# GpSimd multiplies four of the twelve FFN weight units by their signs

## The reference

```python
x = x + 0.5 * ffn(layernorm(x), w_gate_up, w_proj)
x = x + attn(layernorm(x), Wq, Wk, Wv, Wo)      # 32 heads, sliding window of 128
x = x + 0.5 * ffn(layernorm(x), w_gate_up, w_proj)

def ffn(x, w_gate_up, w_proj):                  # 4096 x 512 and 512 x 2048
    gate, up = split(x @ ternary(w_gate_up).T)
    return rms_norm(silu(gate) * up) @ ternary(w_proj).T

def ternary(w):                                 # groups of 64 along a row, in bf16
    scale = clip(mean(abs(w)), 1e-8)            # of each group
    return clip(round(w / scale), -1, 1) * scale
```

## Time and profile before

| | us |
|---|---|
| median of 3 runs | 2083.98 (2083.1 to 2087.64) |
| the profiled execution | 2085.55 |
| its span, first to last instruction | 2083.7 |
| TensorE busy | 1959.7 (94%) |
| VectorE busy | 1637.6 (79%) |
| ScalarE busy | 1471.2 (71%) |
| GpSimd busy | 803.3 (39%) |

### The profile page before, as it was taken

One profiled execution on the slowest core, in us unless ns is written; L12 is line 12 of the kernel. 1 busy time (PEld: TensorE's weight loads), 2 busy tenths in 40 slices (PEclk: granted clock), 3 DMA queues, 4 the chain that ended last, 5 costly groups with the idle time before them and its releaser, 6 DMA issues. The chain is left out here.

```text
span 2083.7 us, 61746 instructions
## 1 busy us (share of the span) xinstructions
PE 1959.7 (94%) x24766; PEld 1429.4 (69%) x25022; DVE 1637.6 (79%) x4144; ACT 1471.2 (71%) x2617; POOL 803.3 (39%) x688
## 2 busy tenths in 40 slices
PE   6578799999999999999999999999999999999778
PEld 4355577777777777777777777777777777777466
DVE  7956788778877888778887888878887888878774
ACT  7746777677776777767776777767776777777672
POOL 1124334443444344444443444444434443433321
PEclk9789899999999999999999999999999999999889
DMA  6324766566665566656774567557664566646650
GB/s 208 132 41 74 122 104 115 93 108 113 121 120 85 102 111 113 113 90 121 118 119 82 97 113 128 107 89 121 120 104 87 103 124 111 115 85 113 117 108 21
DMA packets 760878, 222.23 MB, mean 107 GB/s; under 512 B 745744, under 2 KB 745744, under 8 KB 760080
## 3 DMA queue, kind: packets, MB, share of 16 engines
q1 hardware_dynamic: 760592, 218.26, 58.4%
HBM read 25.17 MB, written 8.39 MB: 16 GB/s over the span
## 5 line engine op out<-in xcount | busy, mean ns | idle before, releaser
L677 ACT ACTIVATE masked<-masked,exp_bias,exp_scale 128x256 f32<-128x256 f32 (+1 forms) x1024 | 503.8, 562 | 8.6
L988 PEld LDWEIGHTS ps_gu<-xt_A,wgu_t 128*128 128x128 bf16 x8192 | 472.0, 99 | 34.8 <-DVE wgu_t L727 7.6
L988 PE MATMUL ps_gu<-xt_A,wgu_t 128*128 128x128 f16 x8192 | 485.2, 220 | 9.7 <-DVE hid L809 5.1
L988 PE MATMUL ps_gu<-xt_C,wgu_t 128*128 128x128 f16 x8192 | 482.1, 220 | 2.1 <-DMA xt_C<-xh 2.1
L988 PEld LDWEIGHTS ps_gu<-xt_C,wgu_t 128*128 128x128 bf16 x8192 | 467.2, 99 | 11.3 <-DMA xt_C<-xh 2.3
L800 DVE TENSOR_TENSOR prob<-masked,prob 128x1024 f16<-128x1024 f32 (+1 forms) x256 | 355.1, 1387 | 9.1 <-ACT prob L700 9.1
L826 DVE CUSTOM_DVE_ANT_0 masked<-ps_s,mask 128x256 f32<-128x256 f32 (+1 forms) x1024 | 336.9, 384 | 1.0 <-PE ps_s L1035 0.9
L800 DVE TENSOR_TENSOR h_lo<-hid,h_hi 128x512 f16<-128x512 f32 x256 | 198.8, 776 | 129.2 <-ACT h_hi L565 128.4
L565 ACT ACTIVATE h_hi<-hid 128x512 f16<-128x512 f32 x256 | 160.4, 627 | 166.0 <-DVE hid L815 155.8
L534 POOL TENSOR_TENSOR acc_C<-acc_C,sq 128x512 f32<-128x512 f32 x95 | 121.2, 1276 | 396.5 <-ACT sq L694 396.5
L1046 PE MATMUL ps_yy<-wp_t,h_lo 128*128 128x512 bf16 x1024 | 263.7, 380 | 0.0
(11 more groups left out here) (163 smaller groups left out, 2269.9 us busy)
## 6 DMA issues: line engine op xcount, KB each, us to landing
stream<-in_L_attn_x_dram SPq DMA_DIRECT2D x32, 256.0 KB, 3.3
pt<-prob SPq DMA_TRANSPOSE x512, 3.2
out_dram<-stream SPq DMA_DIRECT2D x32, 256.0 KB, 2.7
stream<-in_L_ffn_w_gate_up_dram SPq DMA_DIRECT2D x4, 1024.0 KB, 5.6
prob<-in_L_ffn_w_gate_up_dram SPq DMA_DIRECT2D x4, 1024.0 KB, 6.0
stream<-in_L_ffn_w_proj_dram SPq DMA_DIRECT2D x2, 1024.0 KB, 5.1
prob<-in_L_ffn_w_proj_dram SPq DMA_DIRECT2D x2, 1024.0 KB, 5.0
wv<-in_L_attn_Wo_dram SPq DMA_DIRECT2D x1, 1024.0 KB, 7.9
```

The source lines that it names most:

```text
L677: t = act.activation(p, p, ACT.Exp, bias=exp_bias[:, 4 * g + h:4 * g + h + 1], scale=exp_scale[:, 0:1])
L988: t = pe.matmul(bank[:, j * P:(j + 1) * P], wgu_t[:, k, at:at + P], xt[s][:, part, k, :], start=(k == 0 and part == 0), stop=(k == KD - 1 ...
```

## The change

The product with the signs moves into a function `signed(eng, n)` that either engine can issue. GpSimd does it for units 1, 3, 5 and 7, VectorE for the other eight. GpSimd's four stand in its program between the normalising of block 0 (L498) and the maximum of the scales (L504), and count on a semaphore of their own, `w_qp`. All waits on `w_q` go through `units_done(eng, n)`, which waits for both counts. VectorE gets one wait more, ahead of L714 of units 3, 5, 7 and 9: `w_diff` has two buffers, and GpSimd must have read the one that is written over.

```diff
+        POOL_UNITS = (1, 3, 5, 7)
+
+        def units_done(eng, n):
+            pool_has = sum(u <= n for u in POOL_UNITS)
+            need(eng, w_q, n + 1 - pool_has)
+            need(eng, w_qp, pool_has)
+
+        def signed(eng, n):
+            u = UNITS[n]
+            dst = (wgu_t[:, :, u * 512:(u + 1) * 512] if u < NGU else
+                   wp_t[:, :, (u - NGU) * P:(u - NGU + 1) * P])
+            k = dst.shape[1]
+            eng.wait_ge(w_mk, n + 1)
+            eng.wait_ge(w_sgn, 2 * n + 2)
+            return eng.tensor_tensor(out=dst, in0=w_diff[n % 2].rearrange("p (k c) -> p k c", k=k),
+                                     in1=w_sign[n % 3].rearrange("p (k c) -> p k c", k=k), op=ALU.mult)
 ...
             low(xh[:, 1, :], xhat[:, :], xh[:, 0, :], a_xh["A"], 1, g_xl["A"])
+            for n in POOL_UNITS:
+                signed(pool, n).then_inc(w_qp, 1)
             pool.wait_ge(w_gmax, NGU + 1)
 ...
                 if step == 0:
-                    pool.wait_ge(w_q, NTU)
+                    units_done(pool, NTU - 1)
 ...
                 act.wait_ge(w_tr, i + 1)
-                need(act, w_q, i // 2 - 2)
+                units_done(act, i // 2 - 3)
 ...
                 dve.wait_ge(w_grp, n + 1)
+                if n - 2 in POOL_UNITS:
+                    units_done(dve, n - 2)
                 dve.tensor_tensor(out=diff, in0=wide, in1=w, op=ALU.subtract).then_inc(w_dif, 1)
 ...
-                dve.wait_ge(w_mk, n + 1)
-                dve.wait_ge(w_sgn, 2 * n + 2)
-                (the same product as in signed) .then_inc(w_q, 1)
+                if n not in POOL_UNITS:
+                    signed(dve, n).then_inc(w_q, 1)
 ...
-                        pe.wait_ge(w_q, 2 * c + 2)
+                        units_done(pe, 2 * c + 1)
 ...
-            pe.wait_ge(w_q, NTU)
+            units_done(pe, NTU - 1)
```

More of the change, by code:

```diff
@@ L199, in macaron @@
         w_q = sem("w_q")
+        w_qp = sem("w_qp")
         fs_step = sem("fs_step")
```

## The result

The changed kernel takes 2093.79 us (median, 2093.12 to 2095.25), the kernel before 2083.89 (2081.85 to 2087.64): ratio 1.0043, 95% interval 1.0032 to 1.0054. Slower, as forecast; 2091.3 was predicted, between 2085.8 and 2095.5. The profiled executions differ by less than the medians: spans of 2083.7 and 2091.3 us, +7.6, where +7.3 was predicted.

A forecast was written before the change was run, and what follows sets the result against it. VectorE was taken to bound the weight-unit stage, nearly level with the TensorE, ScalarE, GpSimd loop, and TensorE the steady stage. TensorE's 7.3 us later release, added whole to the 2083.98 us median, gave 2091.3 us, range 2085.8 to 2095.5.

The forecast's parts named there:

- Duration of the product: Each GpSimd sign product of 128x2048 bf16 takes 4.05 us, kept between 3.2 and 4.5.
- Exclusion: In the weight units, GpSimd's products hold VectorE out, making its chain 2.46 + 1.45 + 1.45 + 1.24 = 6.6 us later.
- TensorE: L988's gate products wait for GpSimd's products; the last starts at about 81.86 us instead of 74.57, +7.3 us.
- From there to the end: TensorE's +7.3 us passes through ScalarE to GpSimd's last maximum L511 and VectorE's L761, and the steady stage takes it over whole.
- The rival without exclusion: In the weight units VectorE stays free and only the loop through late TensorE costs: +3.2 us, 2087.2; chance 0.07.
- for whole instructions: VectorE and GpSimd shut each other out on SBUF, each let in only when the other's instruction is over.
- The clock: TensorE's clock may slow unit 7's gate product by 1.1 us or shift start-up stretches; upward 0.10, two stretches less 0.07.
- a stretch: One low-clock period of TensorE more or less later in the start-up, 2.6 us either way.
- The sum: Whole kernel: +7.3 us, taking the profiled execution from 2085.55 to 2092.8 and the median from 2083.98 to 2091.3.

The follow-up runs named there:

- the fills: The changed kernel, but GpSimd fills the weights of units 1, 3, 5 and 7 with zeros instead of multiplying; ratio 1.0023 to the kernel before.
- the quarter product: The kernel before, but GpSimd takes 512 of 2048 columns of the sign products of units 3, 5 and 7; ratio 1.0004.
- the idle experiment: The kernel before, with GpSimd also multiplying two bf16 tiles that nobody needs at units 1, 3, 5 and 7; ratio 1.0036.

## Why the prediction was right

- *Duration of the product.* 4.05 us taken from the f16 row by its slope, 4.06 measured. That it fits to 0.01 us is luck: the rows gave 3.2 to 4.5, and the choice was for the nearest row. The f32 figure of the Trainium skill (GPSIMD Engine Reference, Elementwise, side-by-side cycle accounting), 4.50, was too long for bf16.
- *Exclusion.* Unit 1: L738 begins to work at 28.44 + 4.95 - 1.23 = 32.16 (32.13 predicted). Unit 3: 3.35 - 0.68 = 2.67 us of standing. VectorE is 6.5 us late at L738 of unit 8 (82.31 against 75.78), 6.6 predicted; 6.3 at its last product. That the clip is excluded as well was an assumption; the earlier trace rows didn't show it, and the clips of 3.35 and 3.16 us do. The trace of before had it:

```profile
98.03 1.68 DVE L727 TENSOR_TENSOR wp_t<-q,qt 128x2048 bf16<-128x2048 bf16 x1
99.63 0.89 DVE L712 TENSOR_SCALAR k<-k 128x2048 bf16<-128x2048 bf16 x1
```

```profile
97.30 2.67 POOL L493 TENSOR_SCALAR xhat<-stream,mean_var_A,rstd_A 128x512 f32<-128x512 f32 x1
```

  L712 begins to work at 99.63 + 0.89 - 0.68 = 99.84, 0.13 us before GpSimd's end at 99.97. The row above it bounds the rule, though: L727, with two SBUF inputs, stands for only 0.45 us beside the one-input L493 and is through at 99.71, before GpSimd. So "for whole instructions" is shown for GpSimd's instructions with two inputs, not for L493; why, stays open.
- *TensorE.* Releases at 32.41, 48.40, 65.11, 81.83; 81.86 was predicted for the last, about 32.3, 48, 65 for the others.
- *From there to the end.* +7.3 was to be handed on to the last maximum; measured 116.13 - 108.62 = 7.5. In part this is two misses that cancel: ScalarE releases L528 7.8 us late (96.33 against 88.49; the clock, below), and GpSimd's chain from there to L533 is 0.3 us shorter than before. L526 was ready at 88.8 us (88.0), needed at 97.7 (95.6 worked out, without the statistics of block 1 and the last L809 and L815), so its gap cost nothing.
- *The rival without exclusion* came out near its sum too, as far as the fills stand for it: +4.1 measured, the clips' 1.0 in it, +3.2 worked out (its terms as printed add up to 3.3). No product that reads was run without the exclusion, so that the change would not have paid even then is argued, not shown.
- *The clock.* The last gate product took 3.57 us instead of 2.78, 0.8 of the 1.1 allowed; this is in the 7.85 us of ScalarE. The rest of the clock's effect is the spread of the remainder, 5.6 us over these kernels, more than the 2.6 us a stretch that I allowed for one.
- *What missed:* the medians differ by 9.9 us, not 7.3. The sum was made from one profiled execution, 1.7 us above the median of 2083.89, and I carried the difference over unchanged; the profiled execution after (2093.12) was the fastest of its five, 0.7 below their median. These 2.3 us are the whole step from 7.6 to 9.9. Whether they are spread alone stays open.

## What to carry to other kernels

Work moved from VectorE to GpSimd isn't moved beside it where both read SBUF: here each 1.26 us taken off VectorE put 2.5 to 3.7 us of standing onto it. Before such a move look in the trace for one pair of the two engines that overlaps, read how much longer each instruction became, and give GpSimd no more than VectorE's neighbouring instructions with a PSUM input cover; the quarter product held nothing that way, though its gain in the whole isn't shown. Then ask what holds the stage end when the first bound goes: here it was GpSimd's own chain with its two gaps, and mending that was worth 2.8 us of the stage, the quarter product 0.3.

## What the runs showed of the hardware

- Two SBUF inputs on VectorE against a GpSimd product: 4.95 us for 1.22. Against GpSimd's one-input L493: 1.68 for 1.23. Against a GpSimd fill: 1.22, unchanged. The one-input clip: held by both, 4.46 and 1.07 for 0.68. An input from PSUM: 0.68 and 0.69, unchanged.
- A waiting engine gets in at the next boundary: GpSimd's product in the idle experiment got in behind L735 and ahead of the clip that follows it, which then lasted 4.46 us.
- Between an ordinary GpSimd instruction and a partition maximum 5.5 to 6.2 us pass (7.0 once, in the idle experiment), and 7.0 to 7.9 the other way, with no wait to explain them; with the normalising moved, the last maximum ran without.
- Behind the stage end all these kernels run the same instructions, and take 1968.9 to 1974.5 us for them; most of the difference arises in the first 200 us, with the granted clock (0.92 and 0.88 in the first 100). An edit worth 2 us is read in the stage's own timeline more surely than in the medians.
